# Two attention layers and two expert layers: the null key's exponential moved one score exponential later on ScalarE

## The chip, the cores and the metric

The kernel runs on one core of a Trainium2 chip. The metric is the device time of one execution in microseconds (us); a kernel is timed by the median of several executions. The core's engines are TensorE (PE in the profile, its weight loads PEld), VectorE (DVE), ScalarE (ACT), GpSimd (POOL) and SyncE (SP), each with an instruction queue that it works off in order.

## The reference

The input x is (2, 1024, 256). Four residual layers follow one another: two causal attention layers with 16 heads of 64 and one shared key and value per batch entry, then two mixture-of-experts layers (8 experts, 2 chosen, 2 shared ones). Every attention row has one more key in front, the null key, with its own value and bias:

```
k = concatenate([null_k, k]); v = concatenate([null_v, v])
sim = einsum(q, k) * SCALE + concatenate([null_bias, bias])
attn = softmax(where(mask, sim, -big))
out = einsum(attn, v);  x = x + layernorm(out @ Wout) * g_out
```

The change touches only the attention layers, and there only the moment at which exp(null score - row maximum) is computed.

## The kernel before

All five engines run one hand-written schedule. A *slot* `n` is one head of one query tile: there are 512 of them (`N`), 2 layers x 8 tiles x 8 units x 4 heads. A *unit* `u` is four heads (`HU = 4`) of one batch entry and one tile of 128 queries, so slots `4u` to `4u+3`; there are 128 units. Tile `t` (0 to 7 in each layer) has `t+1` blocks of 128 keys, so the work of a slot grows from 128 to 1024 columns, and begins again at unit 64, where the second layer starts. In the code `m, k = divmod(n, 4)`.

For each slot, in software-pipelined order: TensorE computes the scores three slots ahead (lines 1636, 1637); VectorE adds the bias two slots ahead and finds the negated row maximum (line 1233, tiles `biased` and `neg_max`); ScalarE takes the exponential of slot `n+1` (line 816, tile `probs`, row sums into `rows`); TensorE transposes the probabilities of slot `n` (line 1759, banks `tp`), ScalarE evicts their fp16 high half (line 911, `p_hi`) and VectorE the low half (line 1332, `p_lo`); TensorE multiplies with the values one slot later (lines 1426 to 1428, bank `op`).

The null key is handled once for a unit, all four heads together, in tiles of 128 x 4. In the iteration `k == 3` of unit `u`, that is `n = 4u+3`, GpSimd issues in this order:

```python
                    pool.wait_ge(s["probs"], HU * (u + 1))
                    gp.tensor_tensor(d_null[:, :], neg_max[:, u % 2, :], null_of(u), ALU.subtract)\
...
                        query_copy(u + 2)
                    pool.wait_ge(s["p_null"], u + 1)
...
                    gp.tensor_tensor(denom[:, :], rows[:, u % 2, :], p_null[:, :], ALU.add).then_inc(s["denom"], 1)
...
                    gp.tensor_tensor(o_null[:, :, :], null_v[:, :].unsqueeze(1).to_broadcast([P, HU, DH]),
```

Those are `d_null` (line 617), a copy of the query of unit `u+2` for TensorE (line 547, `q_a`), `denom` (line 625) and `o_null` (line 628). ScalarE computes `p_null`, the exponential between `d_null` and `denom` (line 920). VectorE uses `o_null` in `n = 4(u+1)+1`, when it adds it to the unit's output (line 1209, `o_raw`) and inverts `denom` (line 1212); only then may TensorE write the bank `op` for the next unit, and GpSimd scales the output (line 586, `o_n`), which TensorE transposes in `n = 4(u+1)+2` (line 1730).

ScalarE's queue around the change, before it: in iteration `4u+3` the exponential of slot `4u+4`, the query's high half (line 837), `p_hi` of slot `4u+3`, then `p_null` of unit `u`; in iteration `4u+4` the exponential of slot `4u+5`, the eviction of the output projection (line 830, `y_s` or `y_acc`), `p_hi` of slot `4u+4`. In the first tiles of the first layer GpSimd also splits weights (lines 528 to 530) and normalises queries (lines 595 to 599).

Of the kernel before, what the change touches and what calls it, by code (L numbers as in the profile page):

```python
# [25 lines left out]
ACT = mybir.ActivationFunctionType  # L26
# [67 lines left out]
def model(nc, a, out):  # L94
# [3 lines left out]
    with ctx:  # L98
        def sb(name, shape, dt=F32):
            return ctx.enter_context(nc.sbuf_tensor(name, shape, dt))  # L100
# [44 lines left out]
        d_null = sb("d_null", [P, HU])  # L145
        p_null = sb("p_null", [P, HU])
        denom = sb("denom", [P, HU])
        r_den = sb("r_den", [P, HU])
        o_null = sb("o_null", [P, HU, DH])
# [116 lines left out]
        def sems(part, names):  # L266
            return {name: sem(part + "_" + name) for name in names.split()}
# [6 lines left out]
        s = sems("attn", """scores bias biased probs  # L274
                    pt p_hi p_lo pv
                    q_proj q_sq q_ss q_nd q_na q_t q_hi q_lo q_dup wnk null_t null
                    x_st x_rs xn xt xt_hi xt_lo xr_hi xr_lo kv kv_act kv_r kv_d kv_v k_dup kt k_hi k_lo
                    d_null p_null denom r_den o_null o_raw o_n ot ot_hi ot_lo y y_s y_acc
                    y_st y_rs y_n x_new""")
# [53 lines left out]
        for jn, (_, ends_, gain, per) in enumerate(jobs):  # L333
            for hi, lo, at, size in ends_:
                step = min(PIECE, per) if gain is not None else PIECE
                starts = list(range(0, size, step))
                if gain is not None:
                    starts.sort(key=lambda c: (c % per, c // per))
                for c in starts:
                    w = min(step, size - c)  # L340
                    pieces.append((jn, hi[:, c:c + w], lo[:, c:c + w], at + c, w, gain,
                                   (at + c) // per if gain is not None else 0))
            job_end.append(len(pieces))
# [14 lines left out]
        def y_adds(u):  # L358

            T, at_ = divmod(u, UNITS)  # L360
            return T * (UNITS - B) + max(0, at_ - B + 1)
# [36 lines left out]
        NU = N // HU  # L398
# [307 lines left out]
        def _(act):  # L706
            ac = nc.scalar
# [79 lines left out]
            for n in range(FIRST, LAST):  # L787
                m, k = divmod(n, HU)
# [16 lines left out]
                if 0 <= i < N:  # L805

                    w = P * (plan.tile(i) + 1)
                    u = plan.unit(i)
                    act.wait_ge(s["biased"], i + 1)
                    if i == 0:  # L810
                        act.wait_ge(setup["penalty"], 2)
                    if i >= 2:
                        act.wait_ge(s["pt"], plan.groups_done(i - 2))
                    if i % HU == 0 and u >= 2:
                        act.wait_ge(s["denom"], u - 1)
                    ac.activation(probs[:, i % 2, 0:w], biased[:, i % 2, 0:w], ACT.Exp,  # L816
                                  bias=neg_max[:, u % 2, i % HU:i % HU + 1], scale=-1.0,
                                  accum_out=rows[:, u % 2, i % HU:i % HU + 1]).then_inc(s["probs"], 1)
                if k == 0 and 0 <= m - 2 < NU:
                    u = m - 2  # L820
                    act.wait_ge(s["y"], u + 1)
                    if u % UNITS < B:
                        if u >= UNITS:
                            act.wait_ge(s["x_new"], (u // UNITS - 1) * B + u % B + 1)
                        dst = y_acc[:, u % B, :]
                    else:
                        if y_adds(u) >= 2:
                            act.wait_ge(s["y_acc"], y_adds(u) - 1)
                        dst = y_s[:, :]
                    ac.activation(dst, first[:, 0:D], ACT.Copy, scale=1.0 / WS).then_inc(s["y_s"], 1)  # L830
                if k == 3 and 0 <= m + 2 < NU:
                    u = m + 2
# [7 lines left out]
                if k == 1 and 0 <= m + 3 < NU:  # L840
                    u = m + 3
# [62 lines left out]
                for j in range(max(1, len(now))):  # L904
# [7 lines left out]
                            .then_inc(s["p_hi"], 1)  # L912
                    if j == 0:
                        small()
                if k == 3 and 0 <= m < NU:
                    u = m
                    act.wait_ge(s["d_null"], u + 1)
                    if u >= 1:
                        act.wait_ge(s["o_null"], u)
                    ac.activation(p_null[:, :], d_null[:, :], ACT.Exp).then_inc(s["p_null"], 1)  # L920
                if n == N - 2:
                    x_hi(0)
                if n == N + 1:
# [497 lines left out]
        def _(pe):  # L1421
# [178 lines left out]
            for n in range(FIRST, LAST):  # L1600
# [146 lines left out]
                for j in range(max(1, len(now), len(before))):  # L1747
                    if j < len(now):
                        gi = now[j]
                        _, j0, nb = plan.groups[gi]  # L1750
                        if gi == 0:
                            release(3)
                        if gi == 1:
                            pe.wait_ge(setup["vec"], 1)
                        pe.wait_ge(s["probs"], n + 1)
                        if gi >= 2:
                            pe.wait_ge(s["p_lo"], gi - 1)
                        for jj in range(nb):
                            last = te.transpose(tp[gi % 2][:, jj * P:(jj + 1) * P],  # L1759
                                                probs[:, n % 2, (j0 + jj) * P:(j0 + jj + 1) * P], ident[:, :])  # L1760
                        last.then_inc(s["pt"], 1)
                    if j < len(before):
                        pv(before[j])
                    if j == 0:
                        small()
# [35 lines left out]
```

## Time and profile before

| what | value |
|---|---|
| median of 3 runs | 1638.32 us (1638.06 to 1643.91) |
| the profiled execution's own time | 1637.45 us |
| its span, first to last instruction | 1635.6 us |
| mean granted TensorE clock | 0.977 |
| PE busy | 1449.0 us (89%) |
| DVE busy | 1415.8 us (87%) |
| ACT busy | 1164.2 us (71%) |
| POOL busy | 834.8 us (51%) |
| `p_null` instructions | 128, first at 54.9 us, last at 1297.6 us |

The attention layers take the span up to about 1300 us (units 0 to 63 until about 713 us, units 64 to 127 after that); the rest is the expert layers. A busy share is an average over the span. The chain is followed back from the last instruction: at each step to what released it, or to the instruction before it on its engine.

### The profile page before, as it was taken

To read this page: it belongs to the slowest core of one execution; us is meant where nothing else is said; L and a number is where in the kernel's file an instruction comes from. 1 tells how busy PE (TensorE), PEld (TensorE's weight loads), DVE (VectorE), ACT (ScalarE), POOL (GpSimd) and SP (SyncE) were. 2 spreads that over 40 slices of the span, in tenths; PEclk is the share of its full clock that TensorE was granted. 3 is DMA by queue.
4 is the path that set the end of the run, shared out by engine and by line. 5 is a ranking of instruction groups with operands and counts; after the bars stand their busy time and mean duration, and the time that the engine had idled before them with its cause. 6 is when DMAs were issued, how large, how long until landed. Compare 5 with 4: busy or idle time off the path is not lost.

```text
span 1635.6 us, 45305 instructions
## 1 busy us (share of the span) xinstructions
PE 1449.0 (89%) x15552; PEld 1069.0 (65%) x15552; DVE 1415.8 (87%) x3693; ACT 1164.2 (71%) x3093; POOL 834.8 (51%) x1637
## 2 busy tenths in 40 slices
PE   3677778888999999986788999999999989999998
PEld 2455556666777777765666777777778756666665
DVE  5667788999999999977788999999999979888887
ACT  4566777887888888877788898988899723333332
POOL 6767778564545444567765343333332266632222
PEclk9778999999999999999999999999999999999999
DMA  5001221112221222111222212222223000000000
GB/s 156 18 27 53 57 76 53 59 67 72 79 68 65 92 105 79 60 41 40 66 79 68 71 66 73 79 86 92 98 90 120 3 19 28 2 1 1 14 14 27
DMA packets 49953, 96.48 MB, mean 59 GB/s; under 512 B 2922, under 2 KB 26560, under 8 KB 49728
## 3 DMA queue, kind: packets, MB, share of 16 engines
q1 hardware_dynamic: 48420, 92.93, 17.3%
q8 instruction: 128, 2.10, 0.5%
q10 hardware_dynamic: 1308, 0.67, 0.2%
q14 instruction: 97, 0.79, 0.2%
HBM read 91.41 MB, written 2.17 MB: 57 GB/s over the span
## 4 chain that ended last, share of the span: by engine, by line
PE 56%; DVE 21%; issue 6%; ACT 6%; POOL 4%; DVEq 0%; ACTq 0%; POOLq 0%
PE tp L1759 10%; DVE biased L1233 6%; PE sc L1636 5%; DVE p_lo L1332 5%; PE sc L1426 4%; PE sc L1428 4%; PE sc L1427 4%; PE sc L1637 4%; DVE q_a L1265 3%; PE aux L1426 3%; PE op L1426 3%; PE aux L1428 2%; PE aux L1427 2%; PE op L1428 2%; PE op L1427 2%
## 5 line engine op out<-in xcount | busy, mean ns | idle before, releaser
L1332 DVE TENSOR_TENSOR p_lo<-tp,p_hi 128x256 f16<-128x256 f32 (+3 forms) x896 | 427.0, 496 | 76.0 <-ACT p_hi L911 67.1
L1759 PE MATMUL tp<-ident,probs 128*128 128x128 f32 x2304 | 415.6, 280 | 24.3 <-DVE p_lo L1332 20.2
L911 ACT ACTIVATE p_hi<-tp 128x256 f16<-128x256 f32 (+3 forms) x896 | 385.9, 445 | 43.7 <-PE tp L1759 29.5
L816 ACT ACTIVATE probs<-biased,neg_max 128x256 f32<-128x256 f32 (+7 forms) x512 | 395.5, 773 | 16.0 <-DVE neg_max L1233 14.3
L1426 PE MATMUL op<-v_s,p_hi 128*128 128x64 f16 x2304 | 298.2, 194 | 30.7 <-DVE p_lo L1332 18.8
L1636 PE MATMUL sc<-k_a,q_a 128*128 128x512 f16 (+3 forms) x768 | 254.6, 332 | 69.0 <-DVE neg_max L1233 51.3
L1759 PEld LDWEIGHTS tp<-ident,probs 128*128 128x128 f32 x2304 | 264.7, 142 | 68.4 <-issue 30.3
L1428 PE MATMUL op<-v_s,p_lo 128*128 128x64 f16 x2304 | 297.8, 194 | 0.0
L1427 PE MATMUL op<-v_s,p_hi 128*128 128x64 f16 x2304 | 297.8, 194 | 0.0
L1426 PEld LDWEIGHTS op<-v_s,p_hi 128*128 128x128 f16 x2304 | 220.2, 99 | 50.5 <-DVE p_lo L1332 30.3
L1637 PE MATMUL sc<-k_b,q_b 128*128 128x512 f16 (+3 forms) x768 | 242.5, 329 | 0.0
L1427 PEld LDWEIGHTS op<-v_s,p_hi 128*128 128x128 f16 x2304 | 211.8, 99 | 9.9
L1428 PEld LDWEIGHTS op<-v_s,p_lo 128*128 128x128 f16 x2304 | 212.1, 98 | 0.0
L1233 DVE CUSTOM_DVE_ANT_0 biased<-sc,bias,neg_null 128x128 f32<-128x128 f32 (+7 forms) x256 | 205.7, 803 | 2.8 <-PE sc L1637 1.5
L1233 DVE CUSTOM_DVE_ANT_0 biased<-sc,bias,null_t 128x128 f32<-128x128 f32 (+7 forms) x256 | 205.6, 803 | 1.0
L541 POOL TENSOR_TENSOR p_lo<-probs,p_hi 128x512 f16<-128x512 f32 x80 | 92.6, 1158 | 175.5 <-ACT p_hi L785 175.5
L1636 PEld LDWEIGHTS sc<-k_a,q_a 128*128 128x128 f16 x768 | 75.0, 98 | 135.4 <-DVE neg_max L1233 75.0
L547 POOL COPY q_a<-q_b 64x512 f16<-64x512 f16 x128 | 77.4, 604 | 160.4 <-ACT q_b L837 157.9
L586 POOL TENSOR_TENSOR o_n<-o_raw,r_den 128x256 f32<-128x256 f32 x128 | 78.6, 614 | 146.9 <-DVE o_raw L1209 146.3
L785 ACT ACTIVATE p_hi<-probs 128x512 f16<-128x512 f32 x80 | 50.4, 630 | 130.5 <-DVE probs L1114 130.5
L1265 DVE TENSOR_TENSOR q_a<-aux,q_b 64x256 f16<-64x256 f32 x256 | 108.1, 422 | 25.4 <-ACT q_b L837 18.1
L779 ACT ACTIVATE biased<-sc 128x512 f32<-128x512 f32 x80 | 47.7, 596 | 90.4 <-PE sc L1428 90.4
(345 smaller groups left out, 3560.6 us busy)
## 6 DMA issues: line engine op xcount, KB each, us to landing
bias<-rel_table SPq DMA_DIRECT2D x4, 2048.0 KB, 8.5
bias<-in_fside_16xSxS SPq DMA_DIRECT2D x4, 2048.0 KB, 8.6
bias<-rel_table SPq DMA_DIRECT2D x4, 1792.0 KB, 8.1
bias<-in_fside_16xSxS SPq DMA_DIRECT2D x4, 1792.0 KB, 7.1
bias<-rel_table SPq DMA_DIRECT2D x4, 1536.0 KB, 6.1
bias<-in_fside_16xSxS SPq DMA_DIRECT2D x4, 1536.0 KB, 6.7
bias<-rel_table SPq DMA_DIRECT2D x4, 1280.0 KB, 5.7
bias<-in_fside_16xSxS SPq DMA_DIRECT2D x4, 1280.0 KB, 6.2
```

What stands on the lines that cost most here:

```text
L541: gp.tensor_tensor(h_lo[:, en % 4, :], h_f[:, en % 2, :], h_hi[:, en % 4, :], ALU.subtract)\
L816: ac.activation(probs[:, i % 2, 0:w], biased[:, i % 2, 0:w], ACT.Exp, bias=neg_max[:, u % 2, i % HU:i % HU + 1], scale=-1.0, accum_out=row ...
L911: ac.activation(p_hi[:, gi % 4, 0:nb * P], tp[gi % 2][:, 0:nb * P], ACT.Copy)\
L1233: ve.tensor_tensor_reduce(out=biased[:, i % 2, 0:w], in0=sc[i % 2][:, 0:w], in1=bias[:, g % 2, i % HU, 0:w], scale=-1.0, scalar=null_of(u) ...
L1265: ve.tensor_tensor(heads(q_a[DH:P, u % 2, :], e), first[e * DH:(e + 1) * DH, 0:UW].rearrange("p (c q) -> p c q", q=P), heads(q_b[0:DH, u % ...
L1332: ve.tensor_tensor(p_lo[:, gi % 4, 0:nb * P], tp[gi % 2][:, 0:nb * P], p_hi[:, gi % 4, 0:nb * P], ALU.subtract).then_inc(s["p_lo"], 1)
L1426: te.matmul(out_, l_hi, r_hi, start=first, stop=False)
L1427: te.matmul(out_, l_hi, r_lo, start=False, stop=False)
L1428: return te.matmul(out_, l_lo, r_hi, start=False, stop=last)
L1636: te.matmul(o_, q_a[:, u % 2, cols], k_a[layer][:, bt, c0:c0 + cw], start=True, stop=False)
L1637: last = te.matmul(o_, q_b[:, u % 2, cols], k_b[layer][:, bt, c0:c0 + cw], start=False, stop=True)
L1759: last = te.transpose(tp[gi % 2][:, jj * P:(jj + 1) * P], probs[:, n % 2, (j0 + jj) * P:(j0 + jj + 1) * P], ident[:, :])
```

## The change

`p_null` of unit `u` is no longer issued at the end of iteration `4u+3` but in iteration `4u+4`, directly behind the exponential of slot `4u+5`, the second exponential that belongs to unit `u+1` (that of slot `4u+4` was already in front of it). Its waits, on `d_null` of this unit and on `o_null` of the unit before, move with it. No instruction is added or removed, and no other queue is changed.

```diff
@@ -816,6 +816,12 @@
                     ac.activation(probs[:, i % 2, 0:w], biased[:, i % 2, 0:w], ACT.Exp,
                                   bias=neg_max[:, u % 2, i % HU:i % HU + 1], scale=-1.0,
                                   accum_out=rows[:, u % 2, i % HU:i % HU + 1]).then_inc(s["probs"], 1)
+                if k == 0 and 1 <= m <= NU:
+                    u = m - 1
+                    act.wait_ge(s["d_null"], u + 1)
+                    if u >= 1:
+                        act.wait_ge(s["o_null"], u)
+                    ac.activation(p_null[:, :], d_null[:, :], ACT.Exp).then_inc(s["p_null"], 1)
                 if k == 0 and 0 <= m - 2 < NU:
                     u = m - 2
                     act.wait_ge(s["y"], u + 1)
@@ -912,12 +918,6 @@
                             .then_inc(s["p_hi"], 1)
                     if j == 0:
                         small()
-                if k == 3 and 0 <= m < NU:
-                    u = m
-                    act.wait_ge(s["d_null"], u + 1)
-                    if u >= 1:
-                        act.wait_ge(s["o_null"], u)
-                    ac.activation(p_null[:, :], d_null[:, :], ACT.Exp).then_inc(s["p_null"], 1)
                 if n == N - 2:
                     x_hi(0)
                 if n == N + 1:
```

## Rows read from the trace of the kernel before

**Rows 1.** The page: busy time and share of the span; the chain's shares by engine.

```profile
PE 1449.0 (89%) x15552; PEld 1069.0 (65%) x15552; DVE 1415.8 (87%) x3693; ACT 1164.2 (71%) x3093; POOL 834.8 (51%) x1637
...
PE 56%; DVE 21%; issue 6%; ACT 6%; POOL 4%; DVEq 0%; ACTq 0%; POOLq 0%
```

**Rows 2.** Instructions of `p_null`: duration min/median/max; idle before, by releaser (us, times).

```profile
L920 ACT ACTIVATE p_null<-d_null x128: 197/207/223, 54.9 to 1297.6; 128x4 f32<-128x4 f32 x128
...
  ACT p_null L920: 38.4, 75
  POOL d_null L617: 20.9, 19
```

**Rows 3.** Waits of ACT, 50 to 300 us: total, times, longest.

```profile
ACT p_null L920 <- POOL d_null L617: 19.0, 15, 2.2
```

**Rows 4.** Timeline around `p_null` of unit 24: start, duration, instruction, idle before.

```profile
272.99 0.20 ACT L920 ACTIVATE p_null<-d_null 128x4 f32<-128x4 f32 x1 [1.70 <-POOL d_null L617]
...
273.10 0.70 ACT L816 ACTIVATE probs<-biased,neg_max 128x512 f32<-128x512 f32 x1
...
273.81 0.36 ACT L830 ACTIVATE y_s<-sc 128x256 f32<-128x256 f32 x1
273.85 0.62 POOL L628 TENSOR_TENSOR o_null<-null_v,p_null 128x256 f32<-128x256 f32 x1
...
274.07 0.64 ACT L911 ACTIVATE p_hi<-tp 128x256 f16<-128x256 f32 x2
...
274.47 0.76 DVE L1332 TENSOR_TENSOR p_lo<-tp,p_hi 128x256 f16<-128x256 f32 x2 [1.22 <-ACT p_hi L911]
...
275.14 0.42 DVE L1209 TENSOR_TENSOR o_raw<-op,o_null 128x256 f32<-128x256 f32 x1
```

**Rows 5.** The chain in order of time at the same place: start, us, what.

```profile
272.80 0.17 POOL d_null L617
...
273.71 0.06 ACT probs L816
...
274.17 0.28 ACT p_hi L911
```

**Rows 6.** The chain at unit 8, where it leaves ACT again.

```profile
121.91 0.21 ACT p_null L920
...
122.82 0.56 POOL o_null L628
```

**Rows 7.** Timeline around `p_null` of unit 66: the shortest tile, no wait.

```profile
732.29 0.20 ACT L920 ACTIVATE p_null<-d_null 128x4 f32<-128x4 f32 x1
732.39 0.39 ACT L816 ACTIVATE probs<-biased,neg_max 128x128 f32<-128x128 f32 x1
...
732.80 0.39 ACT L830 ACTIVATE y_acc<-sc 128x256 f32<-128x256 f32 x1
...
732.91 0.20 POOL L625 TENSOR_TENSOR denom<-rows,p_null 128x4 f32<-128x4 f32 x1
733.06 0.61 POOL L628 TENSOR_TENSOR o_null<-null_v,p_null 128x256 f32<-128x256 f32 x1
...
733.75 0.42 DVE L1209 TENSOR_TENSOR o_raw<-op,o_null 128x256 f32<-128x256 f32 x1
```

**Rows 8.** Timeline around `p_null` of unit 51, a long tile.

```profile
561.31 0.21 ACT L920 ACTIVATE p_null<-d_null 128x4 f32<-128x4 f32 x1
561.40 1.04 ACT L816 ACTIVATE probs<-biased,neg_max 128x896 f32<-128x896 f32 x1
561.80 0.61 POOL L628 TENSOR_TENSOR o_null<-null_v,p_null 128x256 f32<-128x256 f32 x1
...
566.38 0.41 DVE L1209 TENSOR_TENSOR o_raw<-op,o_null 128x256 f32<-128x256 f32 x1
```

**Rows 9.** Waits of all engines: who waited for whom, us, times, longest.

```profile
POOL o_n L586 <- DVE o_raw L1209: 146.3, 100, 3.1
...
PE sc L1730 <- POOL o_n L586: 5.9, 6, 2.1
```

## The prediction

> **What bounds the kernel now.** I read the page first: TensorE is busy 89% of the span and VectorE 87%, ScalarE 71%, GpSimd 51%; the chain that ended last is on PE for 56%, on DVE for 21%, on ACT for 6% and on POOL for 4% [rows 1]. ScalarE as such is not the bound; what its queue does counts only where somebody waits for it.
>
> Then the instructions of `p_null` [rows 2]. One takes 0.207 us, and there are 128. ACT sat idle in front of 19 of them, 20.9 us in all, until POOL had written `d_null`. In the other direction POOL's `denom` waited 75 times for `p_null`, 38.4 us in all. The waits of ACT say where the first kind lies: 15 of the 19, with 19.0 of the 20.9 us, between 50 and 300 us, the short tiles of the first layer, where POOL is late with weights and queries [rows 3]. The other four lie at 718 to 779 us.
>
> Then the timeline and the chain around single units. At unit 24 ACT idles 1.70 us before `p_null`; 0.11 us after its start the exponential of slot 4u+5 starts, 0.71 us later the projection's eviction `y_s`, then `p_hi`; VectorE has sat idle for 1.22 us when that `p_hi` releases `p_lo` [rows 4]. The chain runs through exactly this: `d_null`, `probs`, `p_hi` [rows 5]. At unit 8 it leaves ACT for POOL (`p_null`, then `o_null`) [rows 6]. I went through all 128 units in this way, by timeline, and count.
>
> **The change part by part.** Nothing is added or removed: 128 instructions change places with the 128 exponentials behind them (the last has none). No DMA moves, and POOL's, DVE's and PE's queues stay as they are.
>
> *What it gives.* Is the score exponential ready before `p_null`? In 126 of 127 units its `neg_max` was done before `p_null` started; at unit 29 it came 0.2 us after. So in the 19 waiting units the exponential, idle until now behind the wait, runs inside it. What follows on ACT comes earlier by the smaller of the wait and the exponential's step, 0.4 us on the shortest tile, 0.71 us at unit 24 [rows 4]. Over the 19 that is about 10.5 us of ACT time. That is the ceiling of the gain, not 20.9: `p_null` still waits for the same `d_null`, and everything behind it on ACT still waits too.
>
> How much of it is on the path? `p_lo` moves with `p_hi`, but `o_raw` behind it needs `o_null` as well, which hangs on POOL, whose times do not change. At unit 24 `o_null` ends at 273.85 + 0.62 = 274.47 and `o_raw` starts at 275.14 [rows 4]: 0.67 us, less the 0.03 us that a release takes, so 0.64 us can be had. Taking for each of the 19 the smaller of step and distance gives 7.2 us. Of those the chain passes through the exponential and `p_hi` as at unit 24 in four: units 13, 17, 24 and 25, with 0.10, 0.60, 0.64 and 0.64 us, together 2.0 us. In seven more it goes from `p_null` to POOL, as at unit 8 [rows 6]; there POOL's `q_a` copy, issued before `denom`, is what counts, and the gain is nothing. In the rest it is not near ACT. I take 2.0 us, with 0 and 7.2 as ends.
>
> In the 109 other units the pair takes the same time in either order, so what follows on ACT neither gains nor loses. Only the exponential itself comes 0.10 us earlier (the start-to-start step that `p_null` costs in front of it [rows 4, 7, 8]), and nobody uses that: TensorE reaches its transposes at least 0.77 us after the exponential has ended, in all 128 units.
>
> *What it costs on ACT.* Unknown is what `p_null` costs between a row-sum read and an eviction from PSUM. The nearest rows bound it: 0.10 us as in front of an exponential [rows 7], its whole 0.207 us if nothing overlaps [rows 2]. The difference over 128 units is 13.7 us of ACT time at most, of which 6% [rows 1], 0.8 us, would be on the path. I take nothing, since every other pair of ACT instructions that I saw overlaps, and keep 0.8 us for the range.
>
> *What it costs behind p_null.* `p_null` now comes later by the step of an exponential where ACT did not wait: 0.41 us on the shortest tile (732.80 - 732.39 [rows 7]), about 1 us at seven blocks [rows 8]. Behind it POOL holds `denom`, `o_null`, the next null score, `y_acc`, `o_n` and the weight pieces; behind those are `o_raw` on DVE and `op` on PE. Cover one is the `q_a` copy: `denom` of unit 66 starts 0.42 us after `p_null` ends (732.91 - 732.49), of which some 0.1 is the release, so 0.3 of 0.41 us are hidden [rows 7]. Cover two is the distance from `o_null` to `o_raw`: 0.08 us at unit 66 (733.75 - 733.67 [rows 7]), but 566.38 - 562.41 = 3.97 us at unit 51 [rows 8]; in tiles of three and more blocks it is at least 1.0 us where the shift is 0.6 or more, and it grows with the tile. So `o_raw` comes late, by some 0.05 us, in unit 66 and three like it (68 to 70): 0.2 us. Cover three is for POOL: with about 0.8 us in each of 109 units `denom` waits up to 85 us longer, but POOL then waits 146.3 us for `o_raw` in front of `o_n` [rows 9], and the longer wait comes out of that one. In nine units POOL has no such idle time to spare (32 and 40, 68, 70, 76 and 78, and the first of each tile in the second layer from 80 to 112); there `o_n` is late by up to 0.7 us, and the transposes that need it come 0.1 to 2.2 us after it. TensorE waited for `o_n` 5.9 us in 6 places [rows 9]. I count 0.3 us for these.
>
> *The sum.* 2.0 - 0.2 - 0.3 = 1.5 us earlier. The profiled execution took 1637.45 us around its span of 1635.6; so it would take 1635.95. The median of the runs is 0.87 us above it, and I forecast by the median: 1638.32 - 1.5 = 1636.8 us.
>
> **The rivals.**
> *Nothing lands.* The four places become POOL's: it is busy for most of the 100 to 300 us stretch, and what DVE gains there it may give back at the next `d_null`. Against it: POOL also waits there for DVE. Time: 1638.3 us. The page Perfetto Trace Analysis of the Trainium skill (Identifying the Most-Contended Engine) would have the engine with the highest occupancy optimized first; by that, a gain on ScalarE is worth nothing, and the sum would be 0. The chain's 6% on ACT speaks for most of this, and its passage at unit 24 against it.
>
> *All lands, and more.* Every saved distance counts: 7.2 us, 1631.1 us; with the full 10.5 us of ACT time 1627.8 us. For it: VectorE idles in front of `p_lo` at such places. Against: in seven of them the chain is POOL's own.
>
> *The new wait decides (slower).* `p_null`, late by an exponential, makes `o_null` late, `o_raw` waits for it and holds `op`. It decides from the point where the step exceeds the cover by `q_a` plus the distance to `o_raw`, 0.41 against 0.3 + 0.08 us at unit 66. If the covers fail in all 32 units of the first two tiles of both layers at some 0.45 us, that is 14 us: 1653 us. The second layer's 16 alone, 7 us, give 1645.5 us. Against it: these covers are measured, and the overrun is hundredths.
>
> **How the numbers follow.** Forecast, about 1.5 us faster, 0.50; nothing lands 0.30; gain towards all of it 0.12, half of it beyond 0.5%; new wait 0.08, most of it beyond. A measurement of this kernel tells about 0.5%, 8.2 us, from no change. So faster 0.06, same 0.88, slower 0.06. The range takes in the ceiling of distances, 7.2 us, at the low end, and at the high end no gain with the 0.8 us of ACT, the 0.5 us behind `p_null` and a third of the new wait's 7 us: 1631 to 1642 us.
>
> **What would show it.** After the change ACT should still wait for `d_null` in front of `p_null`, but about 10 us instead of 20.9, in fewer places. `denom`'s wait for `p_null` should rise from 38.4 us to over 100, and `o_n`'s wait for `o_raw` fall by nearly as much. `o_raw`'s own wait for `o_null`, 0.3 us before, should stay under 2 us; if it grows to several, the slower rival is right. ACT's busy time should stay at 1164 us within 3; the span should differ by less than 5 us. I would be wrong if small shifts in the in-order queues add up over the 128 units.

## The result, and the profile after

The kernel became slightly slower: 1643.01 us median (1639.58 to 1644.75, 20 runs) against 1638.53 us (1635.18 to 1643.91, 20 runs) for the kernel before on the same chips. The ratio is 1.0025, with a 95% interval from 1.0018 to 1.0031; on 1638.5 us that is 4.1 us (2.9 to 5.1). The forecast was 1636.8 us in a range up to 1642 us. The sign was wrong, and the median lies 1 us outside the range; only the class, within 0.5% of before, was the forecast one.

The single profiled executions show little more than half of the loss, 1638.0 us of span against 1635.6. They also differ in TensorE's granted clock in the first 300 us, told at the end. So what follows is read at single places, not from the two spans.

The page after the change (busy time; the chain's shares) answers to [rows 1]:

```profile
PE 1449.9 (89%) x15552; PEld 1069.6 (65%) x15552; DVE 1419.6 (87%) x3693; ACT 1165.3 (71%) x3093; POOL 834.0 (51%) x1637
...
PE 56%; DVE 20%; ACT 7%; issue 6%; POOL 5%; DVEq 0%; ACTq 0%; POOLq 0%
```

ScalarE's busy time grew by 1.1 us, VectorE's by 3.8 us. Nothing was added to VectorE. The instructions of `p_null` after answer to [rows 2]. The lines below the first give idle time (us, times) by what ended it: GpSimd's waits for `p_null`, ScalarE's for `d_null`, and last VectorE's own wait, that of `o_raw` for `o_null`:

```profile
L824 ACT ACTIVATE p_null<-d_null x128: 189/202/208, 54.2 to 1300.0; 128x4 f32<-128x4 f32 x128
...
  ACT p_null L824: 113.7, 93
  POOL d_null L617: 11.0, 16
  DVE o_raw L1209: 2.1, 5
```

All waits after the change (who waited for whom, us, times, longest), of those that answer to [rows 9] and one that the prediction doesn't have:

```profile
POOL denom L625 <- ACT p_null L824: 113.7, 93, 5.1
POOL o_n L586 <- DVE o_raw L1209: 88.6, 85, 3.5
DVE xn L1258 <- POOL rstd L645: 6.8, 11, 1.5
PE sc L1730 <- POOL o_n L586: 5.7, 6, 2.1
```

The same wait in the kernel before:

```profile
DVE xn L1258 <- POOL rstd L645: 4.3, 4, 1.7
```

`denom` waits 75.3 us longer and `o_n` 57.7 us shorter, roughly as forecast. The new thing is small in this list: VectorE waits 11 times, not 4, for `rstd`, the reciprocal root of the layer norm. GpSimd computes it once per query tile, in iteration `n0 - 17` before the tile that starts at slot `n0`. That is the unit with number 3 mod 8, and there it stands behind `o_null` of that unit, with nothing between them but, in the first layer, the two short instructions of the next null score.

At unit 24, on the other hand, the change did what the prediction said. The timeline there, as in [rows 4] (start, duration, instruction, idle before):

```profile
271.25 0.20 ACT L824 ACTIVATE p_null<-d_null 128x4 f32<-128x4 f32 x1 [1.00 <-POOL d_null L617]
271.36 0.37 ACT L836 ACTIVATE y_s<-sc 128x256 f32<-128x256 f32 x1
...
272.12 0.62 POOL L628 TENSOR_TENSOR o_null<-null_v,p_null 128x256 f32<-128x256 f32 x1
...
272.76 0.42 DVE L1209 TENSOR_TENSOR o_raw<-op,o_null 128x256 f32<-128x256 f32 x1
```

From the start of `p_null` to `o_raw` it is 1.51 us, where it was 275.14 - 272.99 = 2.15 us [rows 4]: the predicted 0.64 us is there, and `o_raw` now starts 0.02 us after `o_null` ends. ACT's wait for `d_null` is down from 1.70 to 1.00 us.

The loss is seen at unit 51, which is 3 mod 8. [rows 8] show it before the change, but not what runs between `o_null` and `o_raw`. Lines from the timelines of GpSimd and VectorE there, before:

```profile
553.68 0.42 DVE L1209 TENSOR_TENSOR o_raw<-op,o_null 128x256 f32<-128x256 f32 x1
...
562.81 0.25 POOL L644 TENSOR_SCALAR rstd<-mv 128x2 f32<-128x2 f32 x1
563.14 0.72 POOL L645 TENSOR_TENSOR rstd<-rstd,mhalf 128x2 f32<-128x2 f32 x1
563.88 0.73 POOL L662 TENSOR_TENSOR y_acc<-y_acc,y_s 128x256 f32<-128x256 f32 x1
...
564.66 0.73 DVE L1258 TENSOR_SCALAR xn<-x,mv,rstd 128x256 f32<-128x256 f32 x2
```

And after the change, with ScalarE's `p_null`:

```profile
552.90 0.41 DVE L1209 TENSOR_TENSOR o_raw<-op,o_null 128x256 f32<-128x256 f32 x1
...
561.55 0.20 ACT L824 ACTIVATE p_null<-d_null 128x4 f32<-128x4 f32 x1
...
561.89 0.20 POOL L625 TENSOR_TENSOR denom<-rows,p_null 128x4 f32<-128x4 f32 x1 [1.51 <-ACT p_null L824]
562.04 0.61 POOL L628 TENSOR_TENSOR o_null<-null_v,p_null 128x256 f32<-128x256 f32 x1
...
563.39 0.72 POOL L645 TENSOR_TENSOR rstd<-rstd,mhalf 128x2 f32<-128x2 f32 x1
564.08 0.73 POOL L662 TENSOR_TENSOR y_acc<-y_acc,y_s 128x256 f32<-128x256 f32 x1
...
564.14 1.14 DVE L1258 TENSOR_SCALAR xn<-x,mv,rstd 128x256 f32<-128x256 f32 x2 [0.17 <-POOL rstd L645]
...
566.27 0.41 DVE L1209 TENSOR_TENSOR o_raw<-op,o_null 128x256 f32<-128x256 f32 x1
```

All times are best counted from `o_raw` of the unit before, 553.68 and 552.90. `p_null` starts 1.02 us later, 8.65 instead of 561.31 - 553.68 = 7.63 us after it: the step of the exponential. `rstd` ends 1.03 us later, 11.21 instead of 10.18 us. The first `xn`, which had 564.66 - 563.86 = 0.80 us to spare, starts 11.24 instead of 10.98 us after it, 0.26 us late, and VectorE now stands idle for `rstd`. And the two `xn` take 1.14 us, not 0.73: the first starts 0.06 us after GpSimd's addition into `y_acc` and runs beside it. The next `o_raw` comes 13.37 instead of 12.70 us after the last, 0.67 us late, which is 0.26 + 0.41. The chain of the changed kernel goes through all of it (start, us, what):

```profile
561.66 0.10 ACT p_null L824
...
561.89 0.20 POOL denom L625
562.09 0.56 POOL o_null L628
...
563.39 0.73 POOL rstd L645
...
564.14 0.38 DVE xn L1258
...
564.88 0.40 DVE xn L1258
565.28 1.06 DVE p_lo L1332 x2
566.35 0.34 DVE o_raw L1209
```

I then took the same step, from `o_raw` of the unit before to `o_raw` of this one, in all 15 units of this kind that have `rstd` behind `p_null` (3, 11, 19, ... 115), after less before:

```
-0.29 0.02 0.16 0.70 0.26 0.86 0.67 0.36 -0.05 0.32 0.60 0.70 0.51 0.44 0.38
```

From the third on (the first two lie where ACT waits for `d_null` anyway) they add up to 5.9 us. In these thirteen the granted clock is 1.00 before and after. Unit 123, the only one of the kind with no `rstd` behind it, shows 0.00.

### The profile page after: what moved, and what is told of

It is laid out like the page before. It is cut to its first block, busy times and chain, and to the rows that moved or that the text cites. A ratio compares the mean times of both kernels' runs of the same rounds, so it can differ in the third digit from the quotient of the medians.

```text
span 1638.0 us, 45305 instructions
## 1 busy us (share of the span) xinstructions
PE 1449.9 (89%) x15552; PEld 1069.6 (65%) x15552; DVE 1419.6 (87%) x3693; ACT 1165.3 (71%) x3093; POOL 834.0 (51%) x1637
## 4 chain that ended last, share of the span: by engine, by line
PE 56%; DVE 20%; ACT 7%; issue 6%; POOL 5%; DVEq 0%; ACTq 0%; POOLq 0%
PE tp L1759 10%; DVE biased L1233 6%; PE sc L1636 6%; DVE p_lo L1332 5%; PE sc L1426 4%; PE sc L1428 4%; PE sc L1427 4%; PE sc L1637 4%; DVE q_a L1265 3%; PE aux L1426 3%; PE op L1426 3%; PE aux L1428 2%; PE aux L1427 2%; PE op L1428 2%; PE op L1427 2%
```

## The experiments

The theory (A): the loss lies in one place per tile, where `rstd` is queued behind the later `p_null`. Its rivals: the loss is spread over all units as many small shifts (B), or it belongs to the first 200 us and the clock there (C). For the longer `xn` there are two theories: the two engines get in each other's way on SBUF (P), or the length only reflects when `rstd` arrived (Q). In what follows, the sum of steps at units 3 mod 8 is always the one from the third on, less the kernel before. Differences in us below are ratios times 1638.5 us, with the 95% interval.

**e3, the late place in the one unit only.** The old place is kept for all other units, and in e4, e9 and e10 the condition alone is another:

```diff
+        def late(u):
+            return u % UNITS == 3
...
-                if k == 0 and 1 <= m <= NU:
+                if k == 0 and 1 <= m <= NU and late(m - 1):
...
+                if k == 3 and 0 <= m < NU and not late(m):
+                    u = m
+                    act.wait_ge(s["d_null"], u + 1)
+                    if u >= 1:
+                        act.wait_ge(s["o_null"], u)
+                    ac.activation(p_null[:, :], d_null[:, :], ACT.Exp).then_inc(s["p_null"], 1)
```

> p_null is late, as in the change, only in one unit of eight, the one (3 modulo 8) behind whose o_null GpSimd's rstd is queued; in the other 112 units it keeps its old place. Theory A: it has all of the loss and none of the gain: 4 to 7 us above the kernel before, at 1643 to 1646. Theory B (a cost spread evenly over 128 units): 16 of 128 parts of 4 us, half a microsecond: 1638 to 1640. Theory C: 1637 to 1640.

Measured: 1643.19 us (1642.19 to 1645.37, 8 runs), ratio 1.0028 [1.0018, 1.0038], 4.6 us slower (2.9 to 6.2). Sixteen of 128 moves make the whole loss. The steps at units 3 mod 8 add up to 5.97 us, as after the change. The group of `xn` in this kernel (busy us, mean ns of one, idle before, releaser) has the longer instructions and the longer wait:

```profile
L1268 DVE TENSOR_SCALAR xn<-x,mv,rstd 128x256 f32<-128x256 f32 x32 | 17.5, 588 | 7.0 <-POOL rstd L649 7.0
```

**e4, the late place in all units but that one.** `return u % UNITS != 3`.

> The other way round: p_null is late in the 112 units that are not 3 modulo 8. Theory A: it has the gain in the waiting units without the loss: 1 to 4 us below the kernel before, 1635 to 1638. Theory B: 7 eighths of the loss: 1641 to 1643. Theory C: as the changed kernel, 1642 to 1644, if the early units do it.

Measured: 1637.37 us (1636.01 to 1638.21, 11 runs), ratio 0.9987 [0.9979, 0.9996], 2.1 us faster (0.7 to 3.4). `denom` still waits 101.5 us for the 112 late `p_null`, and the time is no longer for it. The group of `xn`:

```profile
L1268 DVE TENSOR_SCALAR xn<-x,mv,rstd 128x256 f32<-128x256 f32 x32 | 14.8, 505 | 4.4 <-POOL rstd L649 4.3
```

Its steps at units 3 mod 8 add up to 0.00. So the loss is not spread, and B falls. C falls with the steps above: those that make the loss begin at unit 19, after 200 us, at an equal granted clock. The two parts, +4.6 and -2.1, give +2.5 us with some 2.1 us either way, the whole change +4.1 us: they agree within that, and no closer.

**e1, the whole change, with `rstd` issued before GpSimd's wait for `p_null`:**

```diff
                         query_copy(u + 2)
+                    if n % STEP_N == STEP_N - 17 and n // STEP_N + 1 < STEPS:
+                        pool.wait_ge(s["x_st"], n // STEP_N + 2)
+                        link(gp.tensor_scalar(rstd[:, :], mv[:, :, 1], EPS, 0.0, ALU.add, ALU.add))
+                        gp.tensor_tensor(rstd[:, :], rstd[:, :], mhalf[:, 0:B], ALU.pow).then_inc(s["x_rs"], 1)
                     pool.wait_ge(s["p_null"], u + 1)
...
-                    if n == n0 - 17:
+                    if n == n0 - 17 and T < 1:
```

> The changed kernel with one more move: GpSimd issues the layer-norm root rstd (once per tile, in the iteration of the unit whose number is 3 modulo 8) in front of its wait for p_null instead of behind o_null. Theory A (the loss sits in this one place: rstd, queued behind the later p_null, makes VectorE wait before xn): the steps of 0.2 to 0.9 us that the changed kernel loses once per tile at that unit vanish, VectorE waits under 3 us for rstd instead of 6.8, and the time is 4 to 6 us below the changed kernel's 1643, at 1637 to 1639, that is 0 to 2 us from the kernel before. Theory B (the loss is spread over all units, for example what p_null costs on ScalarE between two other instructions, or o_null late for VectorE): 1642 to 1644 as the changed kernel. Theory C (an accident of the first 200 us, weights and loads): also 1642 to 1644.

Measured: 1633.14 us (1630.14 to 1634.75, 5 runs) beside 1639.1 us, ratio 0.996 [0.9946, 0.9974], 6.6 us faster (4.3 to 8.8). The timeline of this kernel at unit 51 has the order, and `xn` at its old length:

```profile
558.63 0.72 POOL L626 TENSOR_TENSOR rstd<-rstd,mhalf 128x2 f32<-128x2 f32 x1
559.32 0.20 POOL L630 TENSOR_TENSOR denom<-rows,p_null 128x4 f32<-128x4 f32 x1
...
560.48 0.73 POOL L667 TENSOR_TENSOR y_acc<-y_acc,y_s 128x256 f32<-128x256 f32 x1
...
561.21 0.73 DVE L1263 TENSOR_SCALAR xn<-x,mv,rstd 128x256 f32<-128x256 f32 x2
```

VectorE's wait for `rstd` is down to 0.7 us in 2 places, and the steps at units 3 mod 8 to -1.57 us in sum. Not every `xn` is short in this kernel: 10 of the 32 are over 0.44 us, up to 0.94, beside the addition or `o_null`. The time is 4 us below what theory A had forecast.

**e2, the same edit on the kernel before.** `p_null` stays in its old place.

> The kernel before with the same move of rstd in front of the wait for p_null, p_null itself left in its old place. It tells how much of the first run's gain is the move's own. Theory A: the kernel before has 4.3 us of VectorE waiting for rstd, in 4 tiles, so it gains up to 4 us: 1634 to 1638. Theory B and C: the same where those waits are not on the path, 1637 to 1639.

Measured: 1632.65 us (1632.24 to 1633.83, 5 runs), ratio 0.9961 [0.9949, 0.9974], 6.4 us faster (4.3 to 8.4). With `rstd` out of the way the change costs at most some 3 us and gains at most some 3: e1 against e2 is +0.2 us, and five runs each can't tell less than that. That the kernel before gains as well says that the wait for `rstd` was there already, 4.3 us in 4 places. But e1 and e2 gain some 6 us, and the steps from the third on show 1.5 of them. Where part of the rest lies is told below.

**e5, the whole change, with the one `y_acc` addition that follows `rstd` moved behind the next `o_n`:**

```diff
+                if k == 1 and 2 <= m <= NU + 1 and m % UNITS == HU:
+                    u = m - 2
+                    pool.wait_ge(s["y_s"], u + 1)
+                    pool.wait_ge(s["y_acc"], y_adds(u) - 1)
+                    y_t = y_acc[:, u % B, :]
+                    gp.tensor_tensor(y_t, y_t, y_s[:, :], ALU.add).then_inc(s["y_acc"], 1)
...
-                if k == 0 and 2 <= m <= NU + 1 and (m - 2) % UNITS >= B:
+                if k == 0 and 2 <= m <= NU + 1 and (m - 2) % UNITS >= B and m % UNITS != HU:
```

> The changed kernel, with GpSimd's addition into y_acc that follows rstd directly (once per tile, 0.72 us) moved behind the next o_n. In the changed kernel the first of the two xn instructions takes up to 0.82 us instead of 0.41 in 13 of 16 tiles, and each of these runs beside that addition. Theory P (the two engines get in each other's way on SBUF while both run): every xn takes 0.40 to 0.45 us again, 13 times 0.4 us or some 5 us are saved, 1637 to 1639 against the changed kernel's 1643; VectorE's wait for rstd stays near 7 us. Theory Q (the longer xn only reflects when rstd arrives): the durations stay, and the time is the changed kernel's, 1642 to 1644.

Measured: 1634.77 us (1631.9 to 1637.24, 11 runs) beside 1638.33 us, ratio 0.9978 [0.9967, 0.9988], 3.6 us faster (2.0 to 5.4). The instructions of `xn` in this kernel (duration min/median/max):

```profile
L1265 DVE TENSOR_SCALAR xn<-x,mv,rstd x32: 406/410/415, 14.8 to 1159.4; 128x256 f32<-128x256 f32 x32
```

In the kernel before:

```profile
L1258 DVE TENSOR_SCALAR xn<-x,mv,rstd x32: 401/408/815, 15.0 to 1160.5; 128x256 f32<-128x256 f32 x32
```

And after the change:

```profile
L1258 DVE TENSOR_SCALAR xn<-x,mv,rstd x32: 401/408/817, 15.1 to 1162.9; 128x256 f32<-128x256 f32 x32
```

And the timeline at unit 51 of e5:

```profile
562.05 0.72 POOL L652 TENSOR_TENSOR rstd<-rstd,mhalf 128x2 f32<-128x2 f32 x1
...
562.81 0.74 DVE L1265 TENSOR_SCALAR xn<-x,mv,rstd 128x256 f32<-128x256 f32 x2 [0.17 <-POOL rstd L652]
```

`xn` waits for `rstd` much as after the change, 0.17 us here as there, and 6.5 us in 11 places in all, where it was 6.8 us in 11. But the pair takes 0.74 us, not 1.14, and the longest of all 32 is 415 ns, not 817. So the length comes from the addition beside it and not from the late `rstd`: Q falls. P holds in that the two engines slow each other; that SBUF is where they meet is not shown.

**e6, the same edit on the kernel before.**

> The kernel before with the same move of the addition alone. There the first xn is long, about 0.8 us, in 7 tiles and 0.5 to 0.63 us in 2. Theory P: all near 0.41 us, 7 times 0.4 and 2 times 0.15 us, about 3 us less: 1635 to 1637. Theory Q: the same as the kernel before, 1638 to 1640. The distance between this run and the one before it is then the waiting part of the change's loss less its gain, 1 to 3 us.

Measured: 1632.95 us (1628.88 to 1634.48, 7 runs), ratio 0.9966 [0.9954, 0.9977], 5.6 us faster (3.8 to 7.5). The steps at units 3 mod 8 add up to -2.59 us, in e5 to +0.61: without the addition beside `xn`, the later `p_null` costs 3.2 us there. No `xn` is long in either kernel, so these 3.2 us are delay alone. With the addition in its old place the later `p_null` costs 5.9 us. The 2.7 us between are the price of the addition. The group of `xn` says the same, 17.5 us busy in e3 and after the change, 14.8 us before the change and in e4, and here:

```profile
L1265 DVE TENSOR_SCALAR xn<-x,mv,rstd 128x256 f32<-128x256 f32 x32 | 11.8, 410 | 4.0 <-POOL rstd L652 3.9
```

**e7, the change with both edits,** `rstd` earlier and the addition later.

> The changed kernel with both moves: rstd in front of the wait for p_null, and the addition behind o_n. Nothing of the layer norm is then behind p_null, nor beside it. Both theories: no more than the 1633.1 us of the first run. Theory P: 6 tiles there still have a long xn beside that addition, so 2 us less, 1630 to 1632.

Measured: 1629.34 us (1625.37 to 1630.96, 5 runs), ratio 0.9947 [0.9934, 0.996], 8.7 us faster than before (6.6 to 10.8). It is the fastest version of the study.

**e8, the kernel before with both edits.**

> The kernel before with both moves, p_null in its old place. If the late p_null has a gain of its own of about 2 us, as the run with seven units of eight suggests, this is 1 to 2 us above the run with both moves on the changed kernel. If that gain needs the old order around rstd, the two are equal, as the first two runs were (1633.1 and 1632.7).

Measured: 1631.2 us (1629.16 to 1632.66, 5 runs), ratio 0.9958 [0.9945, 0.997], 6.9 us faster (4.9 to 9.0). e7 is 1.9 us below it, the size that the change should gain when nothing is behind `p_null`; but the intervals overlap, and five runs each don't settle it. In both the longest `xn` are still 0.85 us, now beside `denom` and `o_null`. The group of `xn` in e7:

```profile
L1270 DVE TENSOR_SCALAR xn<-x,mv,rstd 128x256 f32<-128x256 f32 x32 | 13.2, 456 | 0.7 <-POOL rstd L633 0.6
```

**e9, the late place only where the prediction saw a gain.** `return u in (13, 17, 24, 25)`.

> p_null is late only in units 13, 17, 24 and 25, the four in which the trace of the kernel before had the chain run from d_null through the exponential and p_hi, and to which the prediction gave 0.10, 0.60, 0.64 and 0.64 us. By the prediction's account: 2.0 us below the kernel before, with steps of that size at these units in the trace. Rival, given back: what a unit gains the next one loses, since GpSimd comes no earlier; then the steps are followed by others of the opposite sign within one or two units and the time is within 1 us of the kernel before.

Measured: 1637.35 us (1634.06 to 1638.46, 11 runs) beside 1638.75 us, ratio 0.9989 [0.998, 0.9998], 1.8 us faster (0.3 to 3.3). By the step from `o_raw` to `o_raw`, unit 13 gains 0.11 us, unit 17 0.61 and unit 24 0.66; unit 25 gains 0.22, and unit 26 loses 0.42. That is 1.2 us net for the four.

**e10, the late place in the first four tiles, but not at units 3 mod 8.** `return u % UNITS != 3 and u < 4 * UNITS`.

> p_null is late in units 0 to 31, the short tiles of the first layer, except the four of them that are 3 modulo 8; 28 units. By the run with seven units of eight late in all tiles (1.7 us below the kernel before): if the gain is in the waiting units, this has all of it but a few tenths, 1.2 to 2 us. If it is spread over all units, a quarter, 0.4 us.

Measured: 1636.75 us (1632.89 to 1638.14, 11 runs), ratio 0.9988 [0.9979, 0.9997], 2.0 us faster (0.5 to 3.4), as much as e4 with 112 units. The gain is made in the early units, where ACT waits; the moves in the others are neutral within what these runs can tell.

## Why the prediction was wrong

**The gain, 2.0 us: right in size, in part by luck.** e4, e9 and e10 measure 2.1, 1.8 and 2.0 us, each with its interval clear of zero, if only by 0.3 to 0.7 us. Its places were half right. Units 13, 17 and 24 gave 0.11, 0.61 and 0.66 us (0.10, 0.60 and 0.64 predicted). Unit 25 gave 0.2 of 0.64, and unit 26 gives 0.4 back. With the whole change in, as in e4, e10 and after it, unit 17 gives only 0.20. In its place units 15 (0.97), 16 (0.23) and 21 (0.39) gain, none of which the prediction had among its four. The steps of units 13 to 26 without unit 20 (see below) make 2.2 us together: the sum fits because places that were not foreseen made up for those that gave less. The rival that nothing lands is out, and so is the one that 7.2 us do. Those 7.2 us, the low end of the range, and the 10.5 us of ACT time were also added up too high: counted again from the trace they are about 6.5 and 9.3 us.

**The 109 other units neutral on ACT, nothing for the overlap, and the costs behind `p_null` in the ordinary units, 0.2 and 0.3 us: not contradicted.** ACT's busy time rose by 1.1 us, within the 3 us allowed for. e4 moves 112 of the 128 and gains as much as e10 with its 28. `o_raw` waits 2.1 us in 5 places for `o_null`, a hair above the 2 us that I had allowed. Costs of a few tenths are below what the runs can tell.

**The failed step is in what the change costs behind `p_null`: the list of what GpSimd holds there, and cover three, the wait of `o_n` that was to take up the delay.** The list names `denom`, `o_null`, the next null score, `y_acc`, `o_n` and the weight pieces. `rstd` is not in it: it is there in one unit of eight. The prediction even used such a unit, 51, as its example of ample cover, with 3.97 us from `o_null` to `o_raw` [rows 8]. `rstd`, the addition and two `xn` lie in just these 3.97 us, and `xn` had 0.80 us to spare where `p_null` moved by 1.02. So the sentence that the longer wait "comes out of" that of `o_n` is true of seven units and false of the eighth: there VectorE waits for `rstd` long before GpSimd reaches its idle time in front of `o_n`. The step has no price in the sum and no place in the range. It measures +5.9 us by the trace, 3.2 us of it delay and 2.7 us the collision of `xn` with the addition. With the gain, 5.9 - 2.0 = 3.9 us slower, where 4.1 us were measured. VectorE's 3.8 us of added busy time hold the 2.7 of `xn`; the other 1.1 I did not trace.

**The slower rival** had the right form, a wait behind a later `p_null` that outlasts its cover, but another place: `o_raw`'s wait for `o_null`, which did not become large. Its time, 1645.5 us at the least, was not reached.

**The tests that I had set** were of little use here: the waits of ACT, `denom` and `o_n` and the difference of the spans were all about as forecast, and the kernel still was slower. The prediction's last doubt, small shifts that add up over the 128 units, was not the cause either (e3, e4). None of its tests named the other waits for GpSimd. The one row `xn <- rstd`, 4.3 us to 6.8 us, held the answer.

**The rule on the most-contended engine** (Perfetto Trace Analysis of the Trainium skill, Identifying the Most-Contended Engine), as the prediction applied it, gives 0 for the gain on ScalarE. The runs put the gain at about 2 us. The larger gains, 3.6 to 8.7 us, came with another order of GpSimd's queue, though GpSimd has the lowest busy share, 51%.

**What stays open.** The edits of e1, e2, e5, e6, e7 and e8 gain more than the steps at units 3 mod 8 account for: with the 2 us of the change in e1, e5 and e7, the sums of steps give 3.6, 1.5, 1.4, 2.6, 5.4 and 3.3 us from the third tile on, the runs 6.6, 6.4, 3.6, 5.6, 8.7 and 6.9 us. Between 2 and 5 us lie elsewhere, and the times of e1, e2, e5, e6 and e7 are 0.7 to 3.9 us below what was expected of them. The traces show two places. Units 3 and 11, which these sums leave out, take 1.09 us less each in e1 and in e2, at a granted clock of 0.99 and 0.98 before and 1.00 in both. And the step at unit 12 is 13.89 us at a granted clock of 0.52 in the kernel before, but 11.55 us at 0.85 in e1, e2, e7 and e8, 11.26 us at 0.85 in e6 and 12.72 us at 0.73 in e5. With both places the trace of e2 has 6.0 of its 6.4 us. But the step at unit 12 is short after the change and in e10 as well (11.26 us at 0.83), so it does not belong to the edits on `rstd` and the addition alone, and one trace of a kernel doesn't tell whether it comes back in every execution.

Unit 20 is a like case against the change. Its step is 11.46 to 11.47 us at a granted clock of 1.00 in the kernel before and in e2, e3, e6, e8 and e9, and 12.17 to 13.54 us at 0.75 to 0.93 in the six kernels that have units 15 and 16 late (after the change, e1, e4, e5, e7, e10). TensorE is busy for 8.07 us of this step in e2 and for 10.94 us in e1. So in these traces the lower clock takes back 0.7 to 2.1 us of what the units in front of it gain. Why the clock is lower there is not shown.

## What to carry to other kernels

When an instruction is moved back, write down everything that its readers' engines have queued behind the wait for it, over a whole period of the schedule (here eight units, not one), and who waits for each of these: what comes once in eight units cost three times what the common case had saved. A wait that absorbs the delay in front of one instruction does not protect what stands in the queue ahead of that wait. And an instruction that is 0.3 us late can land beside one of another engine that doubles its length, so look at the neighbours at the new time as well as at the wait.

## What the hardware showed

**A VectorE instruction beside a GpSimd one.** `xn` (128x256, f32, from SBUF to SBUF) takes 0.41 us by itself. If GpSimd's addition (128x256, 0.72 to 0.73 us) has begun before it, it takes up to 0.82 us, the addition still 0.72 to 0.73. Over 0.44 us were 9 of the 32 instructions before, 15 after, and none once the addition was moved (e5, e6). In all 24 cases before and after, `xn` ended 0.87 to 0.88 us after the addition had begun, whether it started 0.06 or 0.38 us behind it: it does not run at a lower rate, it ends at a time that the addition sets. It can also be the other way round. At unit 19 of e1 the addition starts 0.10 us behind the second of two `xn`, and it is the addition that is longer, 0.90 us, while the two `xn` take 0.74 us as usual:

```profile
222.15 0.74 DVE L1263 TENSOR_SCALAR xn<-x,mv,rstd 128x256 f32<-128x256 f32 x2
...
222.57 0.90 POOL L667 TENSOR_TENSOR y_acc<-y_acc,y_s 128x256 f32<-128x256 f32 x1
```

The page "SBUF — State Buffer" of the Trainium skill (Who interferes with whom) has the rule: a `tensor_scalar` on VectorE can enter a mode that takes the port pair shared with GpSimd, and whoever issues first has it for the whole instruction while the other is blocked. The runs agree in the effect, and beside the addition also in who pays, the one that came second. In e7 and e8 it is less plain: the `xn` of 0.85 us start 0.06 us behind the short `denom`, but 0.09 us ahead of `o_null`. The runs don't show that the port is the means.

**TensorE's clock in the first 300 us is not the same from one execution to the next.** The stretch from 150 to 180 us of the kernel before (length, busy time of PE, PEld, DVE, ACT and POOL with counts, granted clock, DMA share, GB/s):

```profile
150.00:180.00 30.00, 21.66 (x197) 16.20 (x198) 18.91 (x63) 17.77 (x63) 19.25 (x41) 0.78 0.09 28
```

And after the change:

```profile
150.00:180.00 30.00, 21.17 (x214) 16.14 (x211) 20.84 (x67) 19.44 (x69) 21.33 (x46) 0.91 0.09 28
```

The mean granted clock is 0.78 of 2.4 GHz before and 0.91 after: a part of each stretch is at 1.2 GHz, a longer one before. `o_raw` of unit 12, in this stretch, comes 2.6 us sooner after `o_raw` of unit 11 (granted clock 0.52 before, 0.83 after). At unit 1 it is 2.2 us the other way (0.75 before, 0.50 after). Such pieces hide part of a 4 us loss in the difference of two single spans, +2.4 us. I did not find what in either execution sets them. The medians over 20 runs and the steps at one kind of unit told what the two spans could not.
